# A recurrent cell and a gated network on one core: the order of the first loads, splits and bias rows

## The chip, the cores and the metric

The kernel runs on one core of one Trainium2 chip. The metric is the device time in microseconds (us) of one execution, the median of several runs. Engines are named as in the profile: PE is TensorE (PEld its weight loads), DVE is VectorE, ACT is ScalarE, POOL is GpSimd, SP is SyncE, which here only issues transfers. SPq and ACTq are the instruction queues of SP and ACT, where their transfers are issued.

## The reference

A gated recurrent cell (GRU) runs over 32 steps of a batch of 128 rows with 256 features; each of its states goes through a gated network whose weights are quantised to three levels, and the result is added to the input.

```python
def cell(h, x):
    gi = x @ W_ih + b_ih
    gh = h @ W_hh + b_hh
    i_r, i_z, i_n = jnp.split(gi, 3, axis=-1)
    h_r, h_z, h_n = jnp.split(gh, 3, axis=-1)
    r = jax.nn.sigmoid(i_r + h_r)
    z = jax.nn.sigmoid(i_z + h_z)
    n = jnp.tanh(i_n + r * h_n)
    h_new = (1.0 - z) * n + z * h
    return (h_new, h_new)
_, hs = jax.lax.scan(cell, cond, swapaxes(x, 0, 1))    # 32 steps
...
gate, up = split(hs @ ternary(w_gate_up).T)            # 256 -> 2 x 1024
hn = rms_norm(silu(gate) * up)
out = x + hn @ ternary(w_proj).T                       # 1024 -> 256
```

## The kernel before

**The work.** Step t needs the state of step t-1, so the steps form one chain. Float32 accuracy comes from split operands: each matrix is rounded to a high part (by a copy on ACT: `wi_hi`, `wh_hi`, `xT_hi`, `st_hi`), and the rest is subtracted into a low part (`wi_lo`, `wh_lo`, `xT_lo`, `st_lo`, on DVE or POOL). A product is three matmul passes: high by high, low by high, high by low. Each pass has two matmuls, since the 256 features lie in two halves of 128. The input weights W_ih are 256 x 768 (reset r, update z and candidate n, 256 columns each), and so are the state weights W_hh. `wi` and `wh` are the places in SBUF into which they are loaded (the trace calls both `work`), in the order r, n, z (`GATES`), 256 KB for each gate of each matrix.

**Biases.** Two rows of the two bias vectors are loaded (`b_rows`, inside a part of `xT_all` that is filled later), summed for r and z on DVE, rounded on ACT into `b_hi` (the trace calls that place `hid_lo`), and split on DVE into `b_split`. A matmul of `neg_ones` with `b_split` then writes a bias into a PSUM bank: `seed_rz` or `bias_rows(..., RZ, ...)` is one matmul of 512 columns, `seed_n` two of 256 (L1039).

**The start.** PE first runs `busy(10)`, ten matmuls of 512 columns on zeros whose result nobody reads. Then step 0 is computed gate by gate: `first_input(i)` multiplies the first input with gate i's W_ih, `first_state(i)` the first state with its W_hh. `cT` is the transposed first state as loaded; its high part is copied by ACT, its low part is subtracted by DVE (L885, semaphore `c_lo`). The waits are semaphores: `wi_hi_ok` and `wh_hi_ok` for the high parts of the weights, `wi_ok` and `wh_ok` for the low ones, `wh_z_ok` for the low part of W_hh's z columns, which POOL makes (L327), and `b_split_ok`, which is 1 when the candidate's bias rows are there and 2 when those of r and z are.

**Steps 0 to 7** (`LEAD` = 8) run before any product of the gated network. In each, PE computes the state products of r, n and z, then the bias and input products of the next step (`seed_rz`, `input_rz`, `input_n_part`), and then transposes the new state in two halves (`ps_t`, `hT_early`). Odd steps use the bank `ps_ffn[2]` for r and z, even ones `ps_rz`. Between the gate functions ACT takes pieces of the quantisation of the network's weights, `q_abs_of(u)` and others, for six blocks u of 512 KB; `ld_w[u]` tells that a block has landed. After step 8 the network's products fill PE between the steps.

**Order.** Every engine's program is written out by hand, and each engine takes its instructions in order. Transfers are issued by SP in the order of its program (biases, six weight pieces, inputs, blocks) and two by ACT (L542 the first input, L543 the first state).

## Time and profile before

| what | us |
|---|---|
| median of 3 runs | 345.35 (344.94 to 345.5) |
| the profiled execution: its own time | 345.16 |
| its span, from the first instruction to the last | 343.4 |
| PE busy | 338.2 (98% of the span) |
| DVE busy | 233.1 (68%) |
| ACT busy | 224.9 (66%) |
| POOL busy | 184.1 (54%) |

The profiled execution took 1.76 us more than its span, and it was 0.19 us shorter than the median. A busy PE is not the same as a PE at its full speed: what a matmul costs is read from the distance of its start to the next one's. The row PEclk of the page shows a granted clock of nine tenths or more in all slices, and a mean of 1.000, but the spacing of the matmuls in the first microseconds is twice that of the later ones, which is the spacing of the lower of the two clocks, 1.2 GHz.

### The profile page before, as it was taken

Reading aid. Unit: us, or ns where it says so; the run is one execution under the profiler, and the core shown is the slowest. Engines: PE = TensorE matmul, PEld = TensorE weight load, DVE = VectorE, ACT = ScalarE, POOL = GpSimd, SP = SyncE. Lnnn points to the kernel's source line nnn. Section 1 sums busy time; section 2 is a strip of 40 time slices with the busy share of each in tenths; the row PEclk is TensorE's granted clock in tenths of the full one; section 3 lists DMA queues with packets and bytes.
Section 4 is the critical chain, followed back from the end, with each engine's and each line's share of the span. In section 5 each row is a group of like instructions: output and inputs, shape, how many; then the busy total and the mean of one; then the engine's idle time right before and its main releaser. Section 6 shows DMA issues by size and latency. Waiting matters only on the chain.

```text
span 343.4 us, 5618 instructions
## 1 busy us (share of the span) xinstructions
PE 338.2 (98%) x2048; PEld 294.4 (86%) x2053; DVE 233.1 (68%) x462; ACT 224.9 (66%) x442; POOL 184.1 (54%) x156
## 2 busy tenths in 40 slices
PE   8999999999999999999999999999999999999996
PEld 4989988888988889888888889888888888888895
DVE  7588787999576556754678554775658555665866
ACT  6778888787755757555766666566565655756662
POOL 2316571465825536255454447454462555799694
PEclk9999999999999999999999999999999999999999
DMA  7995000054001000130001000010000100010101
GB/s 241 299 402 224 2 0 2 0 186 183 1 2 62 2 0 0 71 115 2 0 0 63 0 2 1 1 63 0 2 0 15 48 1 2 0 64 1 59 4 61
DMA packets 7891, 18.72 MB, mean 55 GB/s; under 512 B 564, under 2 KB 4788, under 8 KB 7352
## 3 DMA queue, kind: packets, MB, share of 16 engines
q1 hardware_dynamic: 7176, 17.97, 14.1%
q10 hardware_dynamic: 688, 0.39, 0.4%
q8 instruction: 16, 0.26, 0.3%
q14 instruction: 11, 0.09, 0.1%
HBM read 14.17 MB, written 4.19 MB: 53 GB/s over the span
## 4 chain that ended last, share of the span: by engine, by line
PE 90%; DVE 5%; issue 2%; ACT 1%; DVEq 0%
PE ps_ffn L1126 29%; PE ps_out L1164 16%; PE ps_rz L1028 6%; PE ps_rz L1033 6%; PE ps_rz L1029 6%; PE ps_n L1028 3%; PE ps_n L1033 3%; PE ps_n L1029 3%; PE ps_rz L1126 2%; PE ps_t L1119 1%; PE ps_ffn L1291 1%; PE ps_n L1077 1%; PE ps_ffn L1028 1%; PE ps_ffn L1033 1%; PE ps_ffn L1029 1%
## 5 line engine op out<-in xcount | busy, mean ns | idle before, releaser
L359 POOL TENSOR_TENSOR hid_lo<-work,hid_hi 128x512 fp32r<-128x512 f32 x62 | 81.6, 1316 | 103.5 <-ACT hid_hi L457 99.5
L1126 PE MATMUL ps_ffn<-st_hi,wguT 128*128 128x512 f32 x236 | 93.8, 397 | 0.1
L1126 PE MATMUL ps_ffn<-st_lo,wguT 128*128 128x512 f32 x236 | 92.6, 393 | 0.0
L366 POOL TENSOR_TENSOR sq_sum<-sq_sum,work 128x512 f32<-128x512 f32 x55 | 73.2, 1331 | 1.7 <-ACT work L471 0.6
L748 DVE TENSOR_TENSOR work<-work,ps_ffn 128x512 f32<-128x512 f32 x55 | 37.6, 683 | 31.4 <-ACT work L453 31.3
L457 ACT CAST hid_hi<-work 128x512 fp32r<-128x512 f32 x63 | 38.8, 616 | 23.4 <-DVE work L758 23.4
L1126 PEld LDWEIGHTS ps_ffn<-st_hi,wguT 128*128 128x128 f32 x236 | 44.4, 188 | 8.3 <-DVE work L748 0.7
L1126 PEld LDWEIGHTS ps_ffn<-st_lo,wguT 128*128 128x128 f32 x236 | 44.5, 189 | 7.3
L758 DVE TENSOR_TENSOR work<-work,ps_ffn 128x512 f32<-128x512 f32 x63 | 43.2, 686 | 4.7 <-PE ps_ffn L1126 2.8
L1164 PEld LDWEIGHTS ps_out<-wpT,hid_hi 128*128 128x128 f32 x240 | 35.8, 189 | 3.7
L1164 PE MATMUL ps_out<-wpT,hid_lo 128*128 128x256 f32 x240 | 38.8, 284 | 0.0
L421 ACT ACTIVATE rz<-ps_rz 128x512 f32<-128x512 f32 x24 | 14.3, 596 | 36.9 <-PE ps_rz L1033 36.8
L1164 PE MATMUL ps_out<-wpT,hid_hi 128*128 128x256 f32 x240 | 38.3, 282 | 0.0
L453 ACT ACTIVATE work<-ps_ffn 128x512 f32<-128x512 f32 x55 | 32.3, 587 | 6.8 <-PE ps_ffn L1126 6.5
L687 DVE TENSOR_TENSOR r_hn<-rz,ps_n 128x256 f32<-128x256 f32 x28 | 11.7, 419 | 35.6 <-PE ps_n L1033 35.1
L471 ACT ACTIVATE work<-work 128x512 f32<-128x512 f32 x55 | 34.6, 629 | 0.0
L1164 PEld LDWEIGHTS ps_out<-wpT,hid_lo 128*128 128x128 f32 x240 | 33.0, 191 | 0.4 <-POOL hid_lo L359 0.4
L1028 PE MATMUL ps_rz<-wi_hi,xT_hi 128*128 128x512 f32 x54 | 21.4, 396 | 0.0
L1029 PE MATMUL ps_rz<-wi_lo,xT_hi 128*128 128x512 f32 x54 | 21.2, 392 | 0.0
L322 POOL TENSOR_TENSOR xT_lo<-xT_all,xT_hi 128x256 fp32r<-128x256 f32 x10 | 8.1, 814 | 22.2 <-ACT rz L413 20.0
L1028 PE MATMUL ps_rz<-wh_hi,st_hi 128*128 128x512 f32 (+1 forms) x52 | 19.8, 383 | 0.0
L1029 PE MATMUL ps_rz<-wh_lo,st_hi 128*128 128x512 f32 (+1 forms) x52 | 19.7, 381 | 0.0
(232 smaller groups left out, 713.7 us busy)
## 6 DMA issues: line engine op xcount, KB each, us to landing
out_dram<-o_st SPq DMA_DIRECT2D x7, 512.0 KB, 2.8
xT_all<-in_x_dram SPq DMA_DIRECT2D x1, 3072.0 KB, 16.4
x_ring<-in_x_dram SPq DMA_DIRECT2D x1, 3072.0 KB, 11.2
x_ring<-in_L_ffn_w_gate_up_dram SPq DMA_DIRECT2D x4, 512.0 KB, 9.5
x_ring<-in_L_ffn_w_proj_dram SPq DMA_DIRECT2D x2, 512.0 KB, 11.7
x_ring<-in_x_dram SPq DMA_DIRECT2D x1, 1024.0 KB, 6.0
work<-in_L_cond_W_ih_dram SPq DMA_DIRECT2D x3, 256.0 KB, 4.5
work<-in_L_cond_W_hh_dram SPq DMA_DIRECT2D x3, 256.0 KB, 4.8
```

The costliest lines, as they stand in the source:

```text
L359: nc.gpsimd.tensor_tensor(hid_lo[:, j % RING], hid[:, j % 2], f32(hid_hi[:, j % RING]), ALU.subtract).then_inc(hid_lo_ok, 1)
L366: nc.gpsimd.tensor_tensor(sq_sum[:], sq_sum[:], hid_sq[:, j % 2], ALU.add).then_inc(sq_added, 1)
L453: nc.scalar.activation(sg[:, j % 2], gate_bank(G, j), ACT.Sigmoid).then_inc(sg_ok, 1)
L457: nc.scalar.copy(hid_hi[:, j % RING], hid[:, j % 2]).then_inc(hid_hi_ok, 1)
L471: nc.scalar.activation(hid_sq[:, j % 2], hid[:, j % 2], ACT.Square).then_inc(hid_sq_ok, 1)
L748: nc.vector.tensor_tensor(gsg[:, j % 2], sg[:, j % 2], gate_bank(G, j), ALU.mult).then_inc(gsg_ok, 1)
L758: nc.vector.tensor_tensor(hid[:, j % 2], gsg[:, j % 2], up_bank(G, j), ALU.mult).then_inc(hid_ok, 1)
L1028: pe.matmul(dst, hi[:, k, :], w_hi[:, k, cols], start=False, stop=False, skip_group_check=True)
L1029: pe.matmul(dst, hi[:, k, :], w_lo[:, k, cols], start=False, stop=False, skip_group_check=True)
L1033: mm = pe.matmul(dst, lo[:, k, :], w_hi[:, k, cols], start=False, stop=stop and k == KD - 1, skip_group_check=True)
L1126: mm = pe.matmul(bank, w, group_state(part, G, k), start=(k == 0 and i == 0), stop=(k == KD - 1 and i == 1))
L1164: mm = pe.matmul(ps_out[:, s, :], part[:, j % RING, s * P:(s + 1) * P], wpT[:, j, :], start=(j == 0 and s % 2 == 0 and part is hid_hi), st ...
```

## The change

- SP's first transfer is W_ih's r columns; the transposed first state `cT` comes second, then the other weights as before. The two bias loads move from the head of SP's program to ACT's, behind the first input; `cT` leaves ACT's.
- On ACT the copy of W_ih's r columns goes ahead of the rounding of the r and z bias.
- On DVE the split of the r and z bias goes behind the low part of W_ih's r columns. The low part of the first state moves from DVE to POOL.
- On PE there are eight matmuls on zeros in place of ten. The candidate's bias (`seed_n(0)`) moves into `first_input(0)`, ahead of the pass that needs `wi_lo`; the bias of r and z moves into `first_state(0)`, ahead of the pass that needs `wh_lo`. The bias of r and z for step 2 (`seed_rz(2)`, bank `ps_rz`) moves from behind step 1's products to ahead of step 0's transposes, with a wait on `rz_ok` (ACT has read step 0's z).

```diff
@@ block.sync
                 for to, w, landed in ((wi, w_ih, ld_wi), (wh, w_hh, ld_wh)):
                     sp.dma_start(to[:, :, GATES[i]],
                                  w.rearrange("(k p) n -> p k n", p=P)[:, :, GATES[i]]).then_inc(landed[i], 16)
+                    if i == 0 and to is wi:
+                        sp.dma_start(cT[:], cond_t.rearrange("(k p) b -> p k b", p=P)).then_inc(ld_cT, 16)
...
-            for i, b in enumerate((b_ih, b_hh)):
-                sp.dma_start(b_rows[:, i * G3:(i + 1) * G3], b.partition_broadcast(2)).then_inc(ld_b, 16)
             for i in range(3):
                 load_gate(i)
@@ block.gpsimd
             input_lo(0)
+            pool.wait_ge(h_hi, 1)
+            nc.gpsimd.tensor_tensor(state(st_lo, -1), cT[:], f32(state(st_hi, -1)), ALU.subtract).then_inc(c_lo, 1)
             pool.wait_ge(wh_hi_ok, 3)
@@ block.scalar
             act.dma_start(xT_all[:, :, 0:1, :], xt[:, :, 0:1, :]).then_inc(ld_x0, 16)
-            act.dma_start(cT[:], cond_t.rearrange("(k p) b -> p k b", p=P)).then_inc(ld_cT, 16)
+            for i, b in enumerate((b_ih, b_hh)):
+                act.dma_start(b_rows[:, i * G3:(i + 1) * G3], b.partition_broadcast(2)).then_inc(ld_b, 16)
...
             nc.scalar.copy(both_n(b_hi), both_n(b_all)).then_inc(b_hi_ok, 1)
+            w_ih_hi(0)
             act.wait_ge(b_sum_ok, 1)
             nc.scalar.copy(b_hi[:, RZ], b_all[:, RZ]).then_inc(b_hi_ok, 1)
-            w_ih_hi(0)
             act.wait_ge(ld_cT, 16)
@@ block.vector
-            dve.wait_ge(b_hi_ok, 2)
-            nc.vector.scalar_tensor_tensor(out=b_split[0:2, RZ], in0=f32(b_hi[:, RZ]), scalar=ident[0:2, 1:2],
-                                           in1=b_all[:, RZ], op0=ALU.mult, op1=ALU.subtract).then_inc(b_split_ok, 1)
...
             w_ih_lo(0)
-            dve.wait_ge(h_hi, 1)
-            nc.vector.tensor_tensor(state(st_lo, -1), cT[:], f32(state(st_hi, -1)), ALU.subtract).then_inc(c_lo, 1)
+            dve.wait_ge(b_hi_ok, 2)
+            nc.vector.scalar_tensor_tensor(out=b_split[0:2, RZ], in0=f32(b_hi[:, RZ]), scalar=ident[0:2, 1:2],
+                                           in1=b_all[:, RZ], op0=ALU.mult, op1=ALU.subtract).then_inc(b_split_ok, 1)
             w_hh_lo(0)
@@ block.tensor, first_input
+                if i == 0:
+                    pe.wait_ge(b_split_ok, 1)
+                    seed_n(0)
                 pe.wait_ge(wi_ok, i + 1)
@@ block.tensor, first_state
+                if i == 0:
+                    pe.wait_ge(b_split_ok, 2)
+                    bias_rows(ps_rz[:], RZ, False)
                 if i == 1:
                     seed_rz(1)
@@ block.tensor
-            busy(10)
+            busy(8)
             pe.wait_ge(consts, 5)
             first_input(0, ps_rz[:, 0:D])
-            pe.wait_ge(b_split_ok, 2)
-            bias_rows(ps_rz[:], RZ, False)
             first_state(0, ps_rz[:, 0:D], r_sum)
-            seed_n(0)
...
-                    seed_rz(t + 1)
+                    if t > 1:
+                        seed_rz(t + 1)
                     input_rz(t + 1)
...
                 input_n_part(t + 1, 0)
+                if t == 0:
+                    pe.wait_ge(rz_ok, 1)
+                    seed_rz(2)
                 for k, (ready, done) in enumerate(((h_left, hT_left), (h_ok, hT))):
```

PE at the start of the program, from the matmuls on zeros to the last pass of the r gate, in the kernel before (line, operation, output and inputs, shape of the output):

```order
L1291 MATMUL ps_ffn<-q_keep 128x512 x10
L1302 MATMUL ps_rz<-wi_hi,xT_hi 128x256 x2
L1302 MATMUL ps_rz<-wi_hi,xT_lo 128x256 x2
L1306 MATMUL ps_rz<-wi_lo,xT_hi 128x256 x2
L1039 MATMUL ps_rz<-b_split,neg_ones 128x512
L1317 MATMUL ps_rz<-wh_hi,st_hi 128x256 x2
L1317 MATMUL ps_rz<-wh_hi,st_lo 128x256 x2
L1329 MATMUL ps_rz<-wh_lo,st_hi 128x256 x2
L1039 MATMUL ps_n<-b_split,neg_ones 128x256 x2
```

The same place in the changed kernel:

```order
L1291 MATMUL ps_ffn<-q_keep 128x512 x8
L1302 MATMUL ps_rz<-wi_hi,xT_hi 128x256 x2
L1302 MATMUL ps_rz<-wi_hi,xT_lo 128x256 x2
L1039 MATMUL ps_n<-b_split,neg_ones 128x256 x2
L1309 MATMUL ps_rz<-wi_lo,xT_hi 128x256 x2
L1320 MATMUL ps_rz<-wh_hi,st_hi 128x256 x2
L1320 MATMUL ps_rz<-wh_hi,st_lo 128x256 x2
L1039 MATMUL ps_rz<-b_split,neg_ones 128x512
L1335 MATMUL ps_rz<-wh_lo,st_hi 128x256 x2
```

The two bias writes have moved: the candidate's from the end to the fourth place, that of r and z from the fifth to the eighth.

ACT at the start of the program, before:

```order
L542 DMA xT_all<-in_x_dram 128x2x128
L543 DMA cT<-in_cond_dram 128x2x128
L545 ACT_TABLE_LOAD
L545 ACTIVATE table<-ones 128x1
L449 CAST xT_hi<-xT_all 128x256
L549 CAST hid_lo<-xT_all 2x2x256
L551 CAST hid_lo<-xT_all 2x512
L535 CAST wi_hi<-work 128x2x256
L554 CAST st_hi<-cT 128x2x128
L539 CAST wh_hi<-work 128x2x256
```

and in the changed kernel:

```order
L544 DMA xT_all<-in_x_dram 128x2x128
L546 DMA xT_all<-in_L_cond_b_ih_dram 2x768
L546 DMA xT_all<-in_L_cond_b_hh_dram 2x768
L548 ACT_TABLE_LOAD
L548 ACTIVATE table<-ones 128x1
L451 CAST xT_hi<-xT_all 128x256
L552 CAST hid_lo<-xT_all 2x2x256
L537 CAST wi_hi<-work 128x2x256
L555 CAST hid_lo<-xT_all 2x512
L557 CAST st_hi<-cT 128x2x128
L541 CAST wh_hi<-work 128x2x256
```

ACT issues three transfers in place of two ahead of its table load, and the copy of W_ih's r columns stands ahead of the second bias rounding (L551 before, L555 now).

PE at step 0's transposes, as a difference (with - the kernel before, with + the changed one; L1366 and L1373 are the same line of code):

```order
 L1077 MATMUL ps_ffn<-wi_hi,xT_hi 128x256
 L1077 MATMUL ps_ffn<-wi_lo,xT_hi 128x256
-L1366 MATMUL ps_t<-ident,h_nat 128x128
+L1039 MATMUL ps_rz<-b_split,neg_ones 128x512
+L1373 MATMUL ps_t<-ident,h_nat 128x128
 L1077 MATMUL ps_ffn<-wi_hi,xT_hi 128x256
 L1077 MATMUL ps_ffn<-wi_lo,xT_hi 128x256
```

One matmul of 512 columns now stands between step 1's input products and the first transpose; the same matmul is gone from behind `q_group_sums` in step 1.

## Rows read from the trace of the kernel before

**Rows 1.** The page: busy us (share) by engine; the chain that ended last, by engine.

```profile
PE 338.2 (98%) x2048; PEld 294.4 (86%) x2053; DVE 233.1 (68%) x462; ACT 224.9 (66%) x442; POOL 184.1 (54%) x156
...
PE 90%; DVE 5%; issue 2%; ACT 1%; DVEq 0%
```

**Rows 2.** PE's timeline, 0 to 14 us: start, duration, engine, line, what, count.

```profile
1.45 4.45 PE L1291 MATMUL ps_ffn<-q_keep 128*128 128x512 bf16 x10 [1.45 <-DVE q_keep L856]
5.92 0.77 PE L1302 MATMUL ps_rz<-wi_hi,xT_hi 128*128 128x256 f32 x2
...
6.86 0.40 PE L1306 MATMUL ps_rz<-wi_lo,xT_hi 128*128 128x256 f32 x2
7.09 0.39 PE L1039 MATMUL ps_rz<-b_split,neg_ones 128*128 128x512 f32 x1
7.32 0.40 PE L1317 MATMUL ps_rz<-wh_hi,st_hi 128*128 128x256 f32 x2
...
8.02 0.40 PE L1039 MATMUL ps_n<-b_split,neg_ones 128*128 128x256 f32 x2
8.26 0.40 PE L1302 MATMUL ps_n<-wi_hi,xT_hi 128*128 128x256 f32 x2
...
11.81 0.40 PE L1329 MATMUL ps_rz<-wh_lo,st_hi 128*128 128x256 f32 x2
```

**Rows 3.** ACT's timeline, 0 to 14 us.

```profile
3.98 0.61 ACT L551 CAST hid_lo<-xT_all 2x512 fp32r<-2x512 f32 x1
5.16 0.62 ACT L535 CAST wi_hi<-work 128x512 fp32r<-128x512 f32 x1 [0.57 <-DMA work<-in_L_cond_W_ih_dram]
5.68 0.40 ACT L554 CAST st_hi<-cT 128x256 fp32r<-128x256 f32 x1
6.22 0.62 ACT L539 CAST wh_hi<-work 128x512 fp32r<-128x512 f32 x1
...
12.53 1.05 ACT L511 ACTIVATE q_abs<-x_ring 128x1024 bf16<-128x1024 f32 x1
13.83 0.27 ACT L446 CAST st_hi<-ps_t 128x128 fp32r<-128x128 f32 x1 [0.26 <-PE ps_t L1366]
```

**Rows 4.** DVE's and POOL's timelines, 0 to 14 us.

```profile
3.12 0.68 DVE L862 TENSOR_TENSOR xT_all<-xT_all 2x512 f32<-2x512 f32 x1 [0.80 <-DMA xT_all<-in_L_cond_b_hh_dram]
...
6.88 0.69 DVE L880 TENSOR_TENSOR wh_lo<-work,wh_hi 128x512 fp32r<-128x512 f32 x1
...
3.63 0.76 POOL L322 TENSOR_TENSOR xT_lo<-xT_all,xT_hi 128x256 fp32r<-128x256 f32 x1 [1.03 <-ACT xT_hi L449]
9.94 1.29 POOL L327 TENSOR_TENSOR wh_lo<-work,wh_hi 128x512 fp32r<-128x512 f32 x1 [5.56 <-ACT wh_hi L539]
```

**Rows 5.** SP's timeline: its first transfer and that of W_ih's r columns.

```profile
0.73 0.36 SPq L268 DMA_DIRECT2D xT_all<-in_L_cond_b_ih_dram  x1
...
1.44 0.41 SPq L261 DMA_DIRECT2D work<-in_L_cond_W_ih_dram  x1
```

**Rows 6.** DMA issues at 1.44, 1.89 and 5.98 us: size, us from issue to landing.

```profile
work<-in_L_cond_W_ih_dram SPq DMA_DIRECT2D x1, 256.0 KB, 3.7
...
work<-in_L_cond_W_hh_dram SPq DMA_DIRECT2D x1, 256.0 KB, 4.3
...
x_ring<-in_L_ffn_w_gate_up_dram SPq DMA_DIRECT2D x1, 512.0 KB, 6.5
```

**Rows 7.** Windows: PE, PEld, DVE, ACT, POOL busy, PEclk, DMA share, GB/s.

```profile
3.00:3.50 0.50, 0.50 (x2) 0.15 (x1) 0.38 (x1) 0.49 (x4) 0.00 (x0) 1.00 0.63 164
...
4.50:5.00 0.50, 0.50 (x3) 0.21 (x2) 0.50 (x2) 0.09 (x1) 0.00 (x0) 1.00 0.95 295
```

**Rows 8.** Transposes of steps 0 and 1 on PEld, step 1's new state on DVE.

```profile
13.46 0.14 PEld L1366 LDWEIGHTS ps_t<-ident,h_nat 128*128 128x128 f32 x1 [0.31 <-DVE h_nat L728]
...
18.74 0.14 PEld L1366 LDWEIGHTS ps_t<-ident,h_nat 128*128 128x128 f32 x1
...
18.14 0.48 DVE L715 TENSOR_TENSOR h_nat<-zh,ps_ffn 128x128 f32<-128x128 f32 x2
```

## The prediction
> **What bounds the kernel now.** First the page: PE is busy for 98% of the span, and 90% of the chain that ended last runs through PE [rows 1]. So a microsecond of order on another engine counts only where PE waits for it, and a matmul counts only where it stands in PE's line. The change touches step 0 and two places of steps 0 and 1, so the second view is PE's timeline of the first 14 us [rows 2]. The reader is to see three stretches. From 1.45 us PE works on zeros, ten matmuls in 4.45 us, 0.43 us each. From 5.92 us it does real work, still at that pace (0.21 us for 256 columns); the pair at 6.86 us is the first whose successor starts after 0.23 us, so there the clock rose from 1.2 to 2.4 GHz, although PE had not stood still for more than 0.2 us since 1.45. After that a pair of 256 columns, or one matmul of 512, costs 0.23 to 0.24 us, and I find no gap until the transposes. What starts the real work is seen on ACT: it idled 0.57 us for W_ih's r columns and copied them from 5.16 to 5.78 us [rows 3]; PE followed 0.14 us later. The columns were issued at 1.44 us [rows 5] and took 3.7 us to land [rows 6], that is at 5.14.
>
> The third view answers where PE waits later [rows 8]. Before step 0's first transpose the weight loads idled 0.31 us for DVE's new state. Before step 1's (18.74 us) nothing idled. There the new state was ready earlier: in step 0 PE could start 0.34 us after DVE's pair began (its rows at 13.12 and 13.46 us, of which the second is shown), and in step 1 that pair began at 18.14, so 18.48 was possible and 18.74 was used. Step 1 is bound by PE, with 0.26 us in hand.
>
> **The bias row of step 2.** It is one matmul of 512 columns, 0.23 us by the distance from 7.09 to 7.32 us [rows 2]. Taken out of step 1, it makes PE arrive 0.23 us sooner at the transposes, within the 0.26 us in hand: a gain of 0.23. Put in step 0, it fills 0.23 of the 0.31 us in which the loads idled: cost 0 to 0.05 us, I take 0. Its new wait is for ACT's reading of z, which comes before DVE can make the state and so is always over first.
>
> **The start of the real work.** W_ih's r columns go from 1.44 to 0.73 us [rows 5]. If they land as fast as before, at 4.43, that is 0.71 us of gain, provided ACT is free. ACT now issues three transfers ahead of its table load, some 0.15 us more than two. The bias loads landed 1.97 us after the second one's issue at 1.15 (DVE was let go at 3.12 [rows 4]); issued near 1.6 they land near 3.6, and the first rounding ends its turn near 4.2, still ahead of 4.43. The second rounding (0.61 us [rows 3]) now stands behind the copy, in time in which ACT would wait for W_hh: it takes 4.95 to 5.5, `st_hi` 5.5 to 5.8, and W_hh's r columns, which landed at 1.89 + 4.3 = 6.19, come at 5.8 to 6.0. So PE's first real matmul moves from 5.92 to about 5.2. The eight matmuls on zeros end at 1.45 + 8 x 0.43 = 4.9, so the dropped two cost nothing and would otherwise have stood in the way until 5.75.
>
> **What of that reaches the end of step 0.** PE then works at the lower clock until about 6.85 us, if the clock rises where it did. From 5.2 that is 1.65 us or 7.7 matmuls of 256 columns at 0.213. It has exactly eight to do that need no W_hh: four of the first input, two of the candidate's bias, two with `wi_lo`. They end near 6.9. W_hh's copy, 6.22 to 6.84 before, ends by then at 6.5 to 6.6, so `st_hi`, `st_lo` and the bias of r and z follow at once, 0.7 us; `wh_lo`, ready at 7.57 before [rows 4] and 0.25 to 0.3 earlier now, is there for the last pair. That ends near 7.83, and the candidate's input products start, which before started at 8.26 [rows 2]. Gain: 0.43. With W_ih landing at 4.2 and PE starting at 5.05 it is 0.55; I take **0.48**, inside the two. The same work is done in the same number of matmuls; what is won is that 0.7 us more of it is done before W_hh is ready.
>
> **What must follow.** Each later wait of step 0 must have this much in hand. POOL's `wh_lo` for z ends at 11.23 [rows 4] and is used at 11.81 [rows 2]: 0.58 in hand, plus what the loads gain. POOL also has the first state's low part now, some 0.76 us for 128 x 256 by its row at 3.63 [rows 4] against 0.42 on DVE; from 5.8 to 6.6, before PE asks for it at 7.1 and three us before POOL's next work: 0. DVE's own line only exchanges that for a bias split. The tightest is ACT: `q_abs_of(0)` needs the first block of the gate and up weights, issued at 5.98 and landed 6.5 us later, at 12.48 [rows 6], and ACT started it at 12.53; it holds ACT for 1.05 us, and then `st_hi` of step 0 had 0.26 us in hand [rows 3]. So the gain of step 0 can be no more than 0.26 plus what this block gains. That gain is between the idle time that the earlier issue fills and the issue time: the DMA engines were busy for a share of 0.63 in 3.0 to 3.5 us and of 0.95 in 4.5 to 5.0 [rows 7], which is 0.16 us lost in the one window alone, and SP issues everything after `cT` 0.2 us sooner. I take 0.25, bounds 0.15 and 0.4. The cap is 0.51, and 0.48 passes.
>
> **The sum.** 0.48 + 0.23 = 0.71 us off the profiled execution's 345.16, 344.45. That execution lies 0.19 below the median, so against the median of 345.35 the forecast is 344.65. Nothing behind step 1 is tied to the clock on the wall: the 3 MB of inputs is issued at 16.8 us and used past 40, and the rest of the loads waits for the work itself.
>
> The Trainium skill (DMA: Bandwidth & Descriptors, "Issuing engines are not separate DMA queues") says that transfers issued from two engines share the same 16 DMA engines, so that a second issuer saves only the time of issuing. By this W_ih's r columns now compete with the first input, which was alone in front before. The bytes ahead of their landing fall only by `cT`, 128 KB, and at the 295 KB per us of the window at 4.5 us that is 0.45 us instead of 0.71. PE would start at 5.47, and by the count above the gain of step 0 would be 0.3, the time 344.8. No row here shows the two side by side.
>
> **The rivals.** (1) Most of the gain of step 0 is caught by the loads: W_ih's r columns share the engines with the first input and land near 4.9, or the block for `q_abs_of(0)` comes no sooner. For it: the transfers from 5 us on ran at full share [rows 7]. Against it: the idle share before that. With 0 to 0.3 left, plus 0.23: 344.85 to 345.1. (2) More comes: the clock rises earlier than 5.9 in the typical run, so that PE waits for data alone, or the loads gain 0.4. Then step 0 gains 0.6 to 0.65 and the time is 344.5. (3) Slower: the clock. Between the last zero matmul (4.9) and the first real one PE now stands for 0.3 us or more, and what follows may have holes too. If W_ih's copy comes no sooner than before, the hole is 1 us. If the clock then rises later than 6.85, each us at 1.2 GHz costs 0.5 us of work; from 1.4 us of delay on the gain is gone, and if the clock stayed low once more for the 5.4 us that it did in this trace, 2.7 us would be lost: 346.0 to 347.3. For it: in the trace the clock rose only after 5.4 us of almost unbroken work. Against it: the total of matmuls before 6.85 stays nearly the same.
>
> The Trainium skill (TensorE: Matmul & The Clock Gate, Part 1) says that the point at which the clock rises shifts between runs of the same kernel, depending on where its first matmul falls. The two traces could then differ there by chance; the medians less so. The sum by it would be 0.64 to 0.82, the same within my range.
>
> **How the numbers follow.** The forecast (344.5 to 344.85) has 0.60, rival 1 0.22, rival 2 0.10, rival 3 0.08. About 0.2% of the time, 0.69 us, is what a measurement of this kernel can tell from no change, and my forecast of 0.70 lies at that line. A little over half of its 0.60 counts as faster, with all of rival 2 and little else: faster 0.45. Same: the rest of the forecast and rival 1, 0.48. Slower 0.07, rival 3. The range leaves out rival 3 and the ends: 344.3 to 345.2.
>
> **What would show it.** In the profile of the changed kernel: PE's first real matmul at 5.0 to 5.3 us; its pairs at 0.43 us until the clock rises, then no gap before 7.1; the candidate's input products near 7.8; step 0's first transpose near 13.0 and without the 0.31 us; step 1's near 18.0. Wrong would be: ACT's copy of W_ih's r columns after 4.8 (rival 1), `st_hi` of step 0 waiting behind `q_abs_of(0)`, POOL's low part of the state after 7.1, or pairs at 0.43 us behind 7 us (rival 3).

## The result, and the profile after

The changed kernel takes 346.78 us, the median of 5 runs (346.53 to 347.07), against 345.35 for the kernel before in 5 runs beside it. The ratio is 1.0042, 95% interval 1.0023 to 1.0062: it is slower, by 1.4 us, where 0.7 us faster was forecast. The profiled execution took 346.78 us, of which 344.6 are its span and 2.18 lie outside. Before it was 345.16, with a span of 343.4 and 1.76 outside. So 1.2 us were lost inside the span and 0.4 outside. One profiled execution in this document, that of a_busy10_dve_memset, ran at a granted clock of 0.62 and took 501.58 us; it is left out of that kernel's numbers in the table below, which are those of the nine others.

The page's span, PE's line and the chain that ended last, in the kernel after (compare [rows 1]):

```profile
span 344.6 us, 5614 instructions
...
PE 90%; DVE 4%; issue 2%; ACT 2%; DMA 1%; ACTq 0%; DVEq 0%
```

PE bounds the kernel as before. New in the chain is DMA with 1%: it now runs through the landing of the second bias vector, and from there over ACT to PE's first real matmul at 6.09 us (start, us, what):

```profile
1.87 2.92 DMA xT_all<-in_L_cond_b_hh_dram
...
4.81 0.62 ACT hid_lo L552
5.43 0.53 ACT wi_hi L537
```

Where the time goes is told by one group in two kernels, the transposes of the state that L1119 does from step 8 on (number of them, min/median/max ns, start of the first and of the last). Before:

```profile
L1119 PE MATMUL ps_t<-ident,h_nat x48: 271/273/273, 55.9 to 288.8; 128*128 128x128 f32 x48
```

After:

```profile
L1119 PE MATMUL ps_t<-ident,h_nat x48: 271/272/273, 57.2 to 290.1; 128*128 128x128 f32 x48
```

The first is 1.3 us later and the last is 1.3 us later. So what was lost inside the span was lost before step 8, and after it nothing more was lost or given back. PE's timeline of the first 14 us in the kernel after, to be read against [rows 2]:

```profile
1.45 3.59 PE L1291 MATMUL ps_ffn<-q_keep 128*128 128x512 bf16 x8 [1.45 <-DVE q_keep L859]
6.09 0.77 PE L1302 MATMUL ps_rz<-wi_hi,xT_hi 128*128 128x256 f32 x2 [1.05 <-ACT wi_hi L537]
6.66 0.63 PE L1302 MATMUL ps_rz<-wi_hi,xT_lo 128*128 128x256 f32 x2
...
9.22 0.65 PE L1335 MATMUL ps_rz<-wh_lo,st_hi 128*128 128x256 f32 x2
9.68 0.43 PE L1302 MATMUL ps_n<-wi_hi,xT_hi 128*128 128x256 f32 x2
9.95 0.40 PE L1302 MATMUL ps_n<-wi_hi,xT_lo 128*128 128x256 f32 x2
...
13.26 0.40 PE L1335 MATMUL ps_rz<-wh_lo,st_hi 128*128 128x256 f32 x2
```

The level of the clock is read here and below from the spacing, 0.43 us a pair for the lower and 0.23 to 0.24 for the higher; the granted clock in the windows of these microseconds is 1.00 at both. The reader is to see three things. The real work begins at 6.09 us, not at 5.2 as forecast and not even at 5.92 as before. Ahead of it PE stood for 1.05 us, from the end of the eight zero matmuls. And all real matmuls of the r gate then run at the lower clock, 0.43 us for a pair, up to 9.7 us, where before the clock rose at 6.86. The candidate's input products start at 9.68 instead of 8.26, which is 1.42 us late, and the last pass of z is 1.45 late. Why `wi_hi` came late is on ACT:

```profile
4.26 0.40 ACT L451 CAST xT_hi<-xT_all 128x256 fp32r<-128x256 f32 x1 [0.62 <-DMA xT_all<-in_x_dram]
4.81 0.62 ACT L552 CAST hid_lo<-xT_all 2x512 fp32r<-2x512 f32 x1
5.33 0.61 ACT L537 CAST wi_hi<-work 128x512 fp32r<-128x512 f32 x1
6.05 0.62 ACT L555 CAST hid_lo<-xT_all 2x512 fp32r<-2x512 f32 x1
6.58 0.40 ACT L557 CAST st_hi<-cT 128x256 fp32r<-128x256 f32 x1
6.88 0.61 ACT L541 CAST wh_hi<-work 128x512 fp32r<-128x512 f32 x1
```

and in the first transfers of SP and ACT (start, us of issuing) and their landings (KB, us from issue to landing; SP's W_ih columns, ACT's first input):

```profile
0.73 0.44 SPq L261 DMA_DIRECT2D work<-in_L_cond_W_ih_dram  x1
0.74 0.50 ACTq L544 DMA_DIRECT2D xT_all<-in_x_dram  x1
...
1.87 0.24 ACTq L546 DMA_DIRECT2D xT_all<-in_L_cond_b_hh_dram  x1
...
work<-in_L_cond_W_ih_dram SPq DMA_DIRECT2D x1, 256.0 KB, 3.3
xT_all<-in_x_dram ACTq DMA_DIRECT2D x1, 128.0 KB, 3.5
```

W_ih's columns were there at 0.73 + 3.3 = 4.03 us, 1.1 us sooner than before. But the first input, which before was copied from 3.14 us on, landed only at 4.24, and the biases near 4.8 instead of 3.1. ACT takes them in its order: the first input, the candidate's bias, and only then W_ih's columns, which had waited for 1.3 us. So the transfer that was put first came sooner, and nothing could start with it. (No kernel here copies W_ih's columns ahead of the first input and the bias.) DVE and POOL beside that, in the kernel after (compare [rows 4]):

```profile
4.81 1.20 DVE L865 TENSOR_TENSOR xT_all<-xT_all 2x512 f32<-2x512 f32 x1 [2.49 <-DMA xT_all<-in_L_cond_b_hh_dram]
...
7.21 1.22 DVE L884 SCALAR_TENSOR_TENSOR b_split<-hid_lo,ident,xT_all 2x512 fp32r<-2x512 f32 x1
8.36 0.67 DVE L879 TENSOR_TENSOR wh_lo<-work,wh_hi 128x512 fp32r<-128x512 f32 x1
...
4.74 0.73 POOL L322 TENSOR_TENSOR xT_lo<-xT_all,xT_hi 128x256 fp32r<-128x256 f32 x1 [2.13 <-ACT xT_hi L451]
7.05 0.83 POOL L327 TENSOR_TENSOR st_lo<-cT,st_hi 128x256 fp32r<-128x256 f32 x1 [1.58 <-ACT st_hi L557]
```

The sum of the biases took 1.20 us where it took 0.68, and the second split 1.22. Both ran while POOL subtracted, and each ended 0.54 or 0.55 us after POOL had: 6.01 after 5.47, 8.43 after 7.88. `wh_lo` is 1.5 us later than before (8.36 for 6.88).

What worked as forecast is the bias row of step 2. The transposes of steps 0 and 1 on PEld, after (compare [rows 8]):

```profile
14.90 0.14 PEld L1373 LDWEIGHTS ps_t<-ident,h_nat 128*128 128x128 f32 x1 [0.19 <-DVE h_nat L731]
...
19.94 0.14 PEld L1373 LDWEIGHTS ps_t<-ident,h_nat 128*128 128x128 f32 x1
```

Step 0's is 1.44 us late, step 1's only 1.20: 0.24 was won between them. How much of that a kernel gets depends on what PE finds ahead of step 0's transposes; see b_seed_only below.

### The profile page after: what moved, and what is told of

It is laid out like the page before. It is cut to its first block, busy times and chain, and to the rows that moved or that the text cites. A ratio compares the mean times of both kernels' runs of the same rounds, so it can differ in the third digit from the quotient of the medians.

```text
span 344.6 us, 5614 instructions
## 1 busy us (share of the span) xinstructions
PE 338.5 (98%) x2046; PEld 295.0 (86%) x2051; DVE 233.2 (68%) x461; ACT 224.9 (65%) x442; POOL 185.0 (54%) x157
## 4 chain that ended last, share of the span: by engine, by line
PE 90%; DVE 4%; issue 2%; ACT 2%; DMA 1%; ACTq 0%; DVEq 0%
PE ps_ffn L1126 29%; PE ps_out L1164 16%; PE ps_rz L1028 6%; PE ps_rz L1033 6%; PE ps_rz L1029 6%; PE ps_n L1028 3%; PE ps_n L1033 3%; PE ps_n L1029 3%; PE ps_rz L1126 2%; PE ps_t L1119 1%; PE ps_ffn L1033 1%; PE ps_n L1077 1%; PE ps_ffn L1028 1%; PE ps_ffn L1029 1%; DMA xT_all<-in_L_cond_b_hh_dram 1%
## 5 line engine op out<-in xcount | busy, mean ns | idle before, releaser
L690 DVE TENSOR_TENSOR r_hn<-rz,ps_n 128x256 f32<-128x256 f32 x28 | 11.7, 418 | 35.3 <-PE ps_n L1033 35.1
```

## The experiments

"Before" and "after" are the two kernels; each kernel below is one of them with the edit shown. The kernels of one batch ran on one chip, each batch on another, and share runs of the kernel before, whose median was 345.23, 345.22, 345.24, 345.08 and 345.55 us in the five batches. Where two kernels of different batches are compared below, a tenth or two of their difference may be the chips'. "Outside" is the time of an execution less its span, the median over a kernel's executions; in the kernel before it was 1.8.

| kernel | batch | median us (runs) | ratio to before, 95% interval | span of the profiled one | outside |
|---|---|---|---|---|---|
| a_busy10 | 1 | 346.53 (11) | 1.0037 [1.0026, 1.0049] | 344.4 | 2.15 |
| b_busy8 | 1 | 346.45 (12) | 1.0027 [1.0009, 1.0045] | 345.0 | 1.80 |
| a_loads_before | 1 | 346.86 (10) | 1.0043 [1.0025, 1.0061] | 345.5 | 2.17 |
| b_seed_only | 1 | 345.07 (12) | 1.0004 [0.9987, 1.0022] | 343.1 | 1.83 |
| a_busy10_clo_dve | 2 | 346.04 (8) | 1.0026 [1.0016, 1.0036] | 344.3 | 1.82 |
| b_clo_pool | 2 | 345.54 (12) | 1.0016 [1.0005, 1.0026] | 343.4 | 2.17 |
| b_loads_after | 2 | 347.84 (4) | 1.0079 [1.0066, 1.0092] | 346.3 | 1.79 |
| a_loads_before_busy10_clo_dve | 2 | 345.22 (11) | 1.0003 [0.9993, 1.0013] | 343.3 | 1.84 |
| after_again | 3 | 347.27 (6) | 1.0054 [1.0040, 1.0068] | 345.1 | 2.19 |
| order_wih_first | 3 | 345.74 (11) | 1.0014 [1.0005, 1.0022] | 344.0 | 1.83 |
| b_seed_seedn | 3 | 344.71 (12) | 0.9988 [0.9980, 0.9996] | 343.1 | 1.81 |
| b_pool_memset | 3 | 344.74 (11) | 0.9984 [0.9976, 0.9993] | 343.1 | 1.80 |
| b_clo_pool_dve_memset | 4 | 345.31 (11) | 1.0010 [1.0001, 1.0018] | 344.0 | 1.81 |
| b_pool_sub_small | 4 | 345.14 (11) | 1.0004 [0.9995, 1.0012] | 343.5 | 1.81 |
| b_tile_only | 4 | 344.70 (11) | 0.9991 [0.9978, 1.0004] | 342.7 | 1.80 |
| b_seed_seedn_tile | 4 | 344.49 (12) | 0.9989 [0.9976, 1.0002] | 345.1 | 1.79 |
| a_busy10_dve_memset | 5 | 346.16 (9) | 1.0023 [1.0014, 1.0033] | 344.3 | 1.81 |
| b_seed_seedn_tile_2 | 5 | 344.30 (6) | 0.9967 [0.9955, 0.9979] | 342.6 | 1.83 |

### The zero matmuls and the clock

**a_busy10** is the kernel after with the ten zero matmuls back, **b_busy8** the kernel before with eight.

```diff
-            busy(8)
+            busy(10)
```

> The changed kernel with ten matmuls on zeros again in place of eight, nothing else. Theory 1 (the hole): in the changed kernel PE stood idle from 5.04 to 6.09 us, and its clock rose only near 9.7 us instead of 6.85, which is 2.8 us more at half speed, 1.4 us lost. Ten matmuls end near 5.9, the hole is 0.2 us as in the kernel before, the pairs go to 0.23 us spacing near 7 us and the time is 345.1 to 345.4. Theory 2 (the loads): the splits of step 0 come late because the first input and the biases land 1.1 and 1.7 us later, and PE would stand behind them at either clock: 346.5 to 346.8, with PE gaps before 9 us.

> The kernel before with eight matmuls on zeros in place of ten, loads and order untouched. Theory 1: the hole is 5.04 to 5.92 us, the clock rises 3 us later, step 0 ends 1.3 to 1.5 us later: 346.6 to 346.9. Theory 2: nothing changes, since the real work waits for W_ih's columns until 5.92 in both: 345.3.

PE's timeline in a_busy10:

```profile
1.45 4.34 PE L1291 MATMUL ps_ffn<-q_keep 128*128 128x512 bf16 x10 [1.45 <-DVE q_keep L859]
6.08 0.47 PE L1302 MATMUL ps_rz<-wi_hi,xT_hi 128*128 128x256 f32 x2 [0.29 <-ACT wi_hi L537]
...
9.38 0.40 PE L1302 MATMUL ps_n<-wi_hi,xT_hi 128*128 128x256 f32 x2
```

and in b_busy8:

```profile
6.28 0.77 PE L1302 MATMUL ps_rz<-wi_hi,xT_hi 128*128 128x256 f32 x2 [1.23 <-ACT wi_hi L535]
...
9.40 0.57 PE L1039 MATMUL ps_n<-b_split,neg_ones 128*128 128x256 f32 x2
9.81 0.40 PE L1302 MATMUL ps_n<-wi_hi,xT_hi 128*128 128x256 f32 x2
```

With ten, the hole is 0.29 us and PE has its higher clock from the first real pair on (0.47 us, and the next pair 0.31 later). With eight, a hole of 1.23 us is followed by some 3.4 us at the lower clock. In b_busy8 five executions took 344.8 to 345.4 us and seven 346.4 to 347.3, while of the 32 of the kernel before beside them one reached 347.2, and of all its 142 in this document two. So two zero matmuls fewer do not cost time in each execution; they make those that take 1.2 to 2.1 us more than the five's median of 345.2 more frequent. That all seven had the late clock is an inference: only one of them was profiled (346.84), and there W_ih's columns came 0.36 us later than in [rows 3] as well. In the kernel after the price is 0.25 (346.78 against 346.53) to 0.74 (**after_again**, 347.27, the same kernel in batch 3, where the pairs stayed at 0.43 us until 10.6; 346.6 to 346.8 was expected). The intervals of all three overlap, so the 0.25 is not told from nothing by the medians; in the profiles the candidate's products start 0.30 us apart.

> The changed kernel once more, beside the three others on one chip. If its parts add up as measured so far (late loads about 0.8 us, POOL's instruction 0.36 us outside the span, eight matmuls on zeros 0.1 to 0.3 us), 346.6 to 346.8 and 2.15 us outside the span in every run.

But with ten zero matmuls and the clock up, the kernel after is still 1.3 us slower than before. After 6.4 us PE waits again and again in a_busy10 (of the pairs at 6.68, 7.29, 7.89, 8.44 and 9.04 us each next one starts 0.34 to 0.61 us later, not 0.24), and the candidate's products start at 9.38, only 0.3 sooner. The clock is the smaller part.

### Transfers against order

**a_loads_before** is the kernel after with the transfers of the kernel before; **b_loads_after** is the kernel before with those of after, the reverse of the edit shown.

```diff
             for i, b in enumerate((b_ih, b_hh)):
-                act.dma_start(b_rows[:, i * G3:(i + 1) * G3], b.partition_broadcast(2)).then_inc(ld_b, 16)
+                sp.dma_start(b_rows[:, i * G3:(i + 1) * G3], b.partition_broadcast(2)).then_inc(ld_b, 16)
...
-                    if i == 0 and to is wi:
-                        sp.dma_start(cT[:], cond_t.rearrange("(k p) b -> p k b", p=P)).then_inc(ld_cT, 16)
...
+            act.dma_start(cT[:], cond_t.rearrange("(k p) b -> p k b", p=P)).then_inc(ld_cT, 16)
```

> The changed kernel with the transfers issued as in the kernel before (biases first on SP, first state on ACT); the new order on ACT, DVE, POOL and PE and the eight matmuls on zeros stay. The first input and the biases should land near 3.1 us again. Theory 1: PE still waits for W_ih's columns until 5.9, the hole is 0.9 us, the clock rises late: 346.4 to 346.8. Theory 2: with the loads back the loss is gone: 344.9 to 345.2.

> The kernel before with the transfers issued as in the changed one, nothing else. Theory 2 (the loads): the first input lands at 4.2 instead of 3.1 us and the biases at 4.8 instead of 3.1; DVE's sum takes 1.17 us beside POOL and ends at 5.95, ACT's second rounding ends at 6.6 and only then comes the copy of W_ih's r columns, 1.4 us later than before: 346.4 to 346.8. If the early W_ih columns were worth more than the late biases: below 345.

b_loads_after is the slowest of all, by 2.6 us over before (four executions, 347.67 to 348.12), a full us more than was expected. Its PE:

```profile
7.37 0.47 PE L1303 MATMUL ps_rz<-wi_hi,xT_hi 128*128 128x256 f32 x2 [1.47 <-ACT wi_hi L535]
...
8.94 0.40 PE L1318 MATMUL ps_rz<-wh_hi,st_lo 128*128 128x256 f32 x2
9.18 0.59 PE L1330 MATMUL ps_rz<-wh_lo,st_hi 128*128 128x256 f32 x2
...
12.83 0.40 PE L1303 MATMUL ps_rz<-wi_hi,xT_hi 128*128 128x256 f32 x2
```

In the old order of ACT both bias roundings stand ahead of W_ih's copy, so the late biases hold it until 6.6 us. That is the early part of the loss; the rest is the clock, which shows a second form here: it is high from 7.37 to 9.2, then falls to the lower level for 3.4 us, although PE has worked without a gap since 8.5, and rises again. a_loads_before showed the same after its hole of 1.29 us (high from 6.33, low from 8.2 to 11.7), and so it said nothing on the transfers: eight zero matmuls spoiled it, since its time of 346.86 fitted the theory of the late clock and could not exclude the other. The next pair is without that.

**a_busy10_clo_dve** is after with ten zero matmuls and the subtraction of `c_lo` on DVE, behind the bias split; **a_loads_before_busy10_clo_dve** has the old transfers as well, so that only the order on ACT, DVE and PE is new.

```diff
-            pool.wait_ge(h_hi, 1)
-            nc.gpsimd.tensor_tensor(state(st_lo, -1), cT[:], f32(state(st_hi, -1)), ALU.subtract).then_inc(c_lo, 1)
...
+            dve.wait_ge(h_hi, 1)
+            nc.vector.tensor_tensor(state(st_lo, -1), cT[:], f32(state(st_hi, -1)), ALU.subtract).then_inc(c_lo, 1)
             w_hh_lo(0)
```

> The changed kernel with ten matmuls on zeros and with the low part of the first state back on DVE, behind the bias split. Theory 2a (DVE and POOL collide): in the run with ten matmuls DVE's sum and its second split of the bias rows took 1.17 and 1.22 us instead of 0.68 and 0.73, each while POOL subtracted; with POOL out of the second, the split is 0.73 us, but DVE has 0.42 us more to do, so the r gate ends about as before and the span stays within 0.15 us of 344.4. Theory 3 (outside the span): the changed kernel spends 2.15 us outside its span and the kernel before 1.80, and so does every variant with POOL's additional instruction; if that instruction is the cause, this one shows 1.80 and comes out near 346.1. Theory 2 without the collision: 346.5.

> The changed kernel's order on ACT, DVE and PE alone: the transfers as in the kernel before, ten matmuls on zeros, first state's low part on DVE. What is left of the change is the copy of W_ih's columns ahead of the second bias rounding, the two bias writes of step 0 moved on PE, and the bias row of step 2. Theories 2 and 3: no late load, no collision, no time outside: at most the kernel before, less 0.23 us for the row of step 2 if that gain is real: 344.9 to 345.2. If the second rounding and split, now on ACT's and DVE's line between the weights, delay W_hh's parts by 0.3 us: 345.3 to 345.5.

PE in a_busy10_clo_dve, and then PE and DVE in a_loads_before_busy10_clo_dve:

```profile
9.41 0.40 PE L1302 MATMUL ps_n<-wi_hi,xT_hi 128*128 128x256 f32 x2
```

```profile
8.41 0.40 PE L1301 MATMUL ps_n<-wi_hi,xT_hi 128*128 128x256 f32 x2
...
7.34 0.67 DVE L876 TENSOR_TENSOR wh_lo<-work,wh_hi 128x512 fp32r<-128x512 f32 x1
```

The new transfers cost 346.04 - 345.22 = 0.82 us with all else equal and the clock up in both profiles, where the candidate's products start 1.00 us apart. The new order as a whole neither costs nor gains anything that can be told from zero (ratio 0.9993 to 1.0013, or -0.2 to +0.4 us).

**order_wih_first** is that last kernel with one change: W_ih's r columns are issued by SP ahead of the biases, which stay on SP.

```diff
+                    if i == 0 and to is wi:
+                        for j, b in enumerate((b_ih, b_hh)):
+                            sp.dma_start(b_rows[:, j * G3:(j + 1) * G3], b.partition_broadcast(2)).then_inc(ld_b, 16)
...
-            for i, b in enumerate((b_ih, b_hh)):
-                sp.dma_start(b_rows[:, i * G3:(i + 1) * G3], b.partition_broadcast(2)).then_inc(ld_b, 16)
```

> The kernel with the changed order and the transfers of before that gave 345.22, with one thing moved: W_ih's r columns are issued ahead of the two biases, all three on SP; the first input and the first state stay on ACT. Theory 2b (it is the 256 KB of W_ih beside the first input that make the input and the biases late, not which queue issues the biases): the first input lands near 4.2 us and the biases near 4.5, and the time is 345.8 to 346.1. Theory 2c (the biases were late because they stood behind the first input in ACT's queue): both land before 3.7, W_ih near 4.4, and the time is 344.7 to 345.1.

It is 0.5 us slower than the one without that change, and its ACT, DVE and POOL show why:

```profile
4.31 0.41 ACT L450 CAST xT_hi<-xT_all 128x256 fp32r<-128x256 f32 x1 [1.03 <-DMA xT_all<-in_x_dram]
...
4.62 0.68 DVE L863 TENSOR_TENSOR xT_all<-xT_all 2x512 f32<-2x512 f32 x1 [2.30 <-DMA xT_all<-in_L_cond_b_hh_dram]
5.36 1.08 DVE L866 SCALAR_TENSOR_TENSOR b_split<-hid_lo,ident,xT_all 2x512 fp32r<-2x512 f32 x1
...
4.80 1.08 POOL L323 TENSOR_TENSOR xT_lo<-xT_all,xT_hi 128x256 fp32r<-128x256 f32 x1 [2.19 <-ACT xT_hi L450]
```

The first input is as late as in the kernel after (4.31), though nothing but the 256 KB was put beside it: its landing takes 3.5 us instead of 2.4. The biases, on SP's queue as before and issued 0.5 us later, came 1.5 us later (4.62 for 3.12). So it is not ACT's queue that delays them. What changed ahead of them are W_ih's 256 KB, and, since the second bias is now issued at 1.62 us and `cT` at 1.26, the 128 KB of `cT` too; the two were not separated.

### The first state's low part on POOL

**b_clo_pool** is the kernel before with the subtraction on POOL.

```diff
+            pool.wait_ge(h_hi, 1)
+            nc.gpsimd.tensor_tensor(state(st_lo, -1), cT[:], f32(state(st_hi, -1)), ALU.subtract).then_inc(c_lo, 1)
             pool.wait_ge(wh_hi_ok, 3)
...
-            dve.wait_ge(h_hi, 1)
-            nc.vector.tensor_tensor(state(st_lo, -1), cT[:], f32(state(st_hi, -1)), ALU.subtract).then_inc(c_lo, 1)
```

> The kernel before with the low part of the first state on POOL in place of DVE, nothing else. Theory 3: the span is as before, 343.3, since PE asks for that part late enough, but 2.15 us lie outside it instead of 1.80: 345.55 to 345.6. Theory 2a: POOL's work from 6.1 to 6.9 us meets DVE's low part of W_hh and makes that 1.1 us long instead of 0.69, PE waits 0.2 to 0.3 us for it: span 343.6. Neither: 345.2.

It is 0.32 us slower with the same span, and all 12 executions had 2.13 to 2.23 us outside it where the kernel before has 1.8. In the span most of DVE's gain is eaten, DVE and POOL in b_clo_pool:

```profile
6.39 1.00 DVE L882 TENSOR_TENSOR wh_lo<-work,wh_hi 128x512 fp32r<-128x512 f32 x1
...
5.91 0.93 POOL L327 TENSOR_TENSOR st_lo<-cT,st_hi 128x256 fp32r<-128x256 f32 x1 [1.59 <-ACT st_hi L556]
```

The subtraction of 0.42 us is off DVE, and `wh_lo` takes 1.00 instead of 0.69, ending at 7.39, again 0.55 after POOL's end at 6.84. Four kernels narrow down where the 0.36 us outside come from: a memset of one column on POOL; the same on DVE in place of the subtraction moved to POOL; a small subtraction on POOL behind the same wait; and the memset on DVE in the kernel after with ten zero matmuls. Nobody reads what they write.

```diff
@@ b_pool_memset
+        scratch = sb("scratch", [P, 1])
...
+            nc.gpsimd.memset(scratch[:], 0.0)
             pool.wait_ge(wh_hi_ok, 3)
@@ b_clo_pool_dve_memset and a_busy10_dve_memset, where the subtraction was
+            nc.vector.memset(spare[:], 0.0)
@@ b_pool_sub_small
+            pool.wait_ge(h_hi, 1)
+            nc.gpsimd.tensor_tensor(spare[:], cT[:, 0, :32], f32(state(st_hi, -1))[:, 0, :32], ALU.subtract)
             pool.wait_ge(wh_hi_ok, 3)
```

> The kernel before with one more instruction on POOL, a memset of one column into a tile that nobody reads, behind its first low part. Theory 3: any further instruction in POOL's program costs the 0.36 us outside the span: 2.17 us outside, 345.55. Rival 3a: it was the subtraction with its wait, not the number: 1.80 outside, 345.2.

> The kernel before with the subtraction of the first state's low part on GpSimd, and in its place on VectorE a memset of one column into a tile that nothing reads, so that both engines carry at least as many instructions as in the kernel before. With GpSimd's subtraction alone the profiled execution had 2.17 us outside its span instead of 1.81. Theory 3a (the 0.36 us outside the span come with the instruction that GpSimd has more): 2.15 to 2.2 outside, about 345.5. Theory 3b (they come with the instruction that VectorE has fewer): 1.8 to 1.85 outside, about 345.2.

> The kernel before with a small subtraction (32 columns) on GpSimd behind the same wait for the state's high part, its result read by nobody, VectorE unchanged. Theory 3a (what GpSimd has more, a subtraction that waits for ScalarE, puts 0.36 us outside the span): 2.15 to 2.2 outside, 345.5. Theory 3b (VectorE's missing instruction does it): 1.8 to 1.85 outside, 345.2. If both this and its neighbour show 1.8, only the large subtraction on GpSimd or both changes together do it.

> The changed kernel with its ten zero matmuls back and a memset of one column on VectorE where the change took the subtraction out (its result is read by nobody). The same kernel without the memset took 346.53, with 2.16 us outside the span. Theory 3b (the 0.36 us outside the span come with VectorE's missing instruction): 1.8 to 1.85 outside and 346.1 to 346.3, the span unchanged near 344.4, since VectorE's longer operations are still there. Its rival (the changed kernel has them for another reason than the kernel before with that move alone): 2.15 to 2.2 and 346.5.

One instruction more on POOL leaves 1.8 outside, with or without the wait. The large subtraction on POOL leaves 1.8 too as soon as DVE has an instruction in its place. So the 0.36 us need DVE's missing instruction, and that holds in the kernel after as well: 346.16 for 346.53, with the span as it was (344.3 for 344.4). Whether they need POOL's large subtraction too is open, since no kernel here has one DVE instruction fewer without it. What happens in those 0.36 us lies outside the profile, and stays open too.

### The bias rows on PE, and a tile

**b_seed_only** is the kernel before with `seed_rz(2)` moved as in the change; **b_seed_seedn** moves `seed_n(0)` too, but leaves the bias of r and z of step 0 where it was; **b_tile_only** has a tile of one column that nothing uses; **b_seed_seedn_tile** has all three, and was run twice.

```diff
@@ b_seed_only, b_seed_seedn
-                    seed_rz(t + 1)
+                    if t > 1:
+                        seed_rz(t + 1)
...
+                if t == 0:
+                    pe.wait_ge(rz_ok, 1)
+                    seed_rz(2)
@@ b_seed_seedn, in first_input and behind first_state(0, ...)
+                if i == 0:
+                    pe.wait_ge(b_split_ok, 1)
+                    seed_n(0)
                 pe.wait_ge(wi_ok, i + 1)
...
-            seed_n(0)
@@ b_tile_only
         ones = sb("ones", [P, 1])
+        scratch = sb("scratch", [P, 1])
```

> The kernel before with one thing moved: the bias row of r and z for step 2 goes ahead of step 0's transposes. Both theories: it fills 0.23 of the 0.31 us in which PE waited for DVE, and step 1 is 0.23 us shorter: 345.1. If the transposes of step 0 are pushed by as much as step 1 gains, 345.35.

> The kernel before with two moves on PE and nothing else: the bias row of step 2 ahead of step 0's transposes, and the candidate's bias of step 0 ahead of the pass that needs W_ih's low part. Theory: the first gives 0.2 us; the second gives another 0.24 in runs where the clock rose before 5.9 us, since PE then waits for that low part, and nothing where it rose near 6.9: 344.8 to 345.0. Rival: the second only moves the wait to W_hh, whose columns land when they land: 345.05 as with the first move alone.

> The kernel before with one unused tile of a column allocated where the memset kernel had it, and no instruction more: every later tile lies 4 bytes further on in each partition. Theory 4a (the memset kernel was 0.5 us faster, 344.74, because the tiles behind lie elsewhere): 344.6 to 344.9. Theory 4b (it was the instruction on GpSimd, or which chip ran it): 345.1 to 345.4.

> The kernel before with the two moves of bias rows on TensorE (step 2's bias row of r and z behind step 1's new gate, step 0's bias row of n ahead of the first W_ih products; 344.71 alone) and the unused tile. Theory 4a: both gains add, 344.1 to 344.4, the fastest of all. Theory 4b: 344.6 to 344.9, as without the tile.

> The same kernel as b_seed_seedn_tile again, on what may be another chip, to tell its ratio to the kernel before (0.9989, interval to 1.0002) from 1: 344.3 to 344.6 and a ratio of 0.998 to 0.999 if the two moves on TensorE and the tile are what made it faster, 345 if it was chance.

`seed_rz(2)` alone gives 0.16 us in the medians, which is not told from zero by its interval. Its profile shows why it gives less than 0.24: there PE's weight loads waited 0.34 us, up to 12.36, for `xT_lo` (POOL's subtraction took 0.97 us beside DVE's `zh`) and came to step 0's transposes without idle time, so that the bias row was not hidden; the distance to step 1's transposes is 5.15 us, against 5.28 before and 5.04 after. Both moves give 0.53, and that is told from zero: ratio 0.9988. With the tile it is 344.49 and 344.30, the second time clear of noise (ratio 0.9967), and the fastest of all kernels here. The tile alone gave 0.38, and the memset on POOL, which brought the same tile, 0.50. The tile moves every later one by 4 bytes. The interval of the tile alone still holds 1, but the profiles show more than the medians. In b_tile_only the 48 transposes from step 8 on are at:

```profile
L1120 PE MATMUL ps_t<-ident,h_nat x48: 270/272/273, 55.6 to 288.1; 128*128 128x128 f32 x48
```

From the first to the last it is 232.5 us, where it is 232.9 before and after. In all four kernels with that tile it is 232.5 to 232.6, in the fifteen others 232.8 to 232.9 (a_busy10_dve_memset is left out), also in the two of these that have an unused tile behind all the others. So some 0.3 us of the gain come in steps 8 to 31 and go with where tiles lie. No view here shows which instruction gets faster, and why it does is not shown.

The profile of b_seed_seedn_tile was an execution with a late clock, 346.93 us, while eleven others took 344.1 to 345.2. Its ACT and PE:

```profile
5.87 0.62 ACT L536 CAST wi_hi<-work 128x512 fp32r<-128x512 f32 x1 [1.32 <-DMA work<-in_L_cond_W_ih_dram]
...
6.64 0.77 PE L1303 MATMUL ps_rz<-wi_hi,xT_hi 128*128 128x256 f32 x2 [0.74 <-ACT wi_hi L536]
...
10.98 0.40 PE L1310 MATMUL ps_n<-wi_lo,xT_hi 128*128 128x256 f32 x2
```

and PE of the same kernel in b_seed_seedn_tile_2:

```profile
5.76 0.47 PE L1303 MATMUL ps_rz<-wi_hi,xT_hi 128*128 128x256 f32 x2
...
8.21 0.40 PE L1310 MATMUL ps_n<-wi_lo,xT_hi 128*128 128x256 f32 x2
```

In one execution W_ih's columns landed 0.7 us later than before, PE stood 0.74 us behind its ten zero matmuls, and the pairs were at 0.43 us until about 10.6: the candidate's `wi_lo` pass is 2.8 us later, and the whole 2.5. The same kernel without a hole had the high clock at 5.76. So what b_busy8's edit does can also come by chance, with a late transfer.

## Why the prediction was wrong

The 1.4 to 2.0 us come apart into four terms, each the difference of two kernels' distances from the kernel before of their own batch: new order 0.00, new transfers +0.82, `c_lo` on POOL +0.48 (0.33 of it outside the span), eight zero matmuls +0.13 to +0.73. That they add up to the 1.43 and 2.03 us of the kernel after in its two measurements proves nothing, since each difference begins at the kernel at which the last one ends. The transfers are the largest term that is clear of noise; the order of the terms could shift some tenths between them. Step by step:

**"W_ih's r columns go from 1.44 to 0.73 us"** and land at 4.43: right, and sooner than forecast, 4.03. The prediction's second estimate, 0.45 us of gain by the bytes ahead (landing near 4.7), erred on the other side. ACT's third transfer was put at 0.15 us and cost 0.42 (its table load starts at 2.14 instead of 1.72), which did not matter: ACT then idled 0.62 us for the first input.

**"The bias loads ... issued near 1.6 they land near 3.6"**: this failed, and it is the step that decided. The forecast had ACT free for the copy of W_ih's r columns at 4.2; it came to it at 5.33. The second bias was issued at 1.87 and took 2.9 us, and so let DVE go at 4.8. The 1.97 us of landing was read from a trace in which 128 KB and one bias of 6 KB had been issued ahead, and was carried to one in which W_ih's 256 KB, `cT`'s 128 KB and W_hh's 256 KB (at 1.73) had been as well. The first input was not costed at all. I took its copy at 3.14 for given, though the first input now had W_ih's 256 KB beside it, and it landed at 4.24. The windows of the kernel after show where that time is (columns as in [rows 7]):

```profile
2.00:2.50 0.50, 0.50 (x3) 0.15 (x1) 0.32 (x2) 0.36 (x1) 0.39 (x2) 1.00 0.48 139
...
3.00:3.50 0.50, 0.50 (x2) 0.15 (x1) 0.00 (x0) 0.49 (x2) 0.00 (x0) 1.00 1.13 357
```

From 3.0 us the engines are full, 357 KB per us where before they moved 164 [rows 7], which is the idle share that I had meant to use. What used it was W_ih's columns and what stands behind them, at the cost of 140 KB that were needed first. The Trainium skill (DMA: Bandwidth & Descriptors, "Issuing engines are not separate DMA queues") says that transfers interleave on the same 16 DMA engines whichever engine issued them. The runs agree: in order_wih_first, with the biases on SP's queue, the second took 3.0 us to land, and 2.9 from ACT's in the kernel after. I weighed it for the large transfer only. It was the small ones that paid.

**"The dropped two cost nothing"**: failed. They bridged the wait until the first copy. The forecast had the hole at 0.3 us; since the start came at 6.09, it was 1.05. That condition stood in rival 3 ("If W_ih's copy comes no sooner than before, the hole is 1 us"), and two of the forecast's own signs of being wrong came true, the copy after 4.8 and pairs at 0.43 us behind 7. Rival 3's size of 346.0 to 347.3 holds the result, but by luck: it was made of the clock alone, and with the clock up a_busy10 still takes 346.53. Its chance of 0.08 was too small, since I left out the loads that make the hole. The Trainium skill (TensorE: Matmul & The Clock Gate, Part 1) says that the rise shifts between runs of one kernel. The two profiles of b_seed_seedn_tile agree, with the higher clock from 5.76 and from about 10.6. What it adds up to is not chance alone, though, as the share of executions above 346.3 us went from 1 of 32 to 7 of 12 in b_busy8.

**"DVE's own line only exchanges that for a bias split"**, POOL at 0: failed twice. The exchange leaves DVE 0.49 us longer in the split, which is what the subtraction took away (0.42), and the bias split now stands ahead of `wh_lo`. In every trace here each DVE instruction of 512 columns with both inputs in SBUF that started during one of POOL's subtractions ended 0.53 to 0.58 us after it (the `zh` of step 0, 256 columns, 0.27 to 0.41): 1.20, 1.22, 1.00 and 1.08 us in the rows shown, for work that takes 0.67 to 0.73 us otherwise. `r_hn` and `n_pre`, which read PSUM, kept their 0.42 us beside it. With POOL silent (a_busy10_clo_dve) the split took 0.73. The Trainium skill (SBUF — State Buffer, "Who interferes with whom") states this as a lock: a VectorE instruction with two inputs in SBUF and a GpSimd instruction that reads SBUF contend for a shared port, which one of them holds while the other waits. The rows agree, in the other direction too: in order_wih_first POOL's subtraction started behind DVE's and took 1.08 us, where it takes 0.72 or 0.73 with DVE idle. The 0.76 of [rows 4], by which the forecast priced it, has a little of this wait in it. I had looked up what POOL's instruction costs and not what it does to its neighbour. The 0.36 us outside the span could not have been read from any row.

**"They end near 6.9"**, and step 0 gains 0.43 to 0.55: failed. The r gate is the same work in the same number of matmuls, but all of it ran at the lower clock, from 6.09 to 9.68, so the arithmetic of the forecast and of rival 1 fell with its start. The clock's rise at 6.86 was also one trace's: in nine of the other profiles with ten zero matmuls the higher clock is there from the first real pair. With the old transfers and the new order (a_loads_before_busy10_clo_dve) the candidate's products start 3.32 us after ACT began to copy W_ih's r columns (8.41 and 5.09), and 2.73 in b_seed_seedn (7.68 and 4.95), which has two of PE's three moves and nothing of ACT's and DVE's. So these two moves were worth 0.53 us in the medians, and the rest of the new order took it back. What did is argued and not tested by itself: on ACT the second rounding stands ahead of W_hh's copy (6.44 us, and 5.78 in b_seed_seedn), and on DVE the second split stands ahead of `wh_lo` (7.34, and 6.54).

**The cap by ACT's `q_abs_of(0)`** was not tested in the kernel after, since nothing came early enough.

**The bias row of step 2**: right in mechanism and size in the kernel after, 0.24 in the traces against 0.23; in the kernel before alone it gave 0.13 by the same distance.

## What to carry to other kernels

A large transfer that is put first can delay the small ones that share its moment, here from either queue; list what the first instruction of each engine needs, and let those bytes go ahead of the large ones. Dummy matmuls ahead of the first real one should reach up to it: count them to the latest arrival of the data, not to the expected one. Before work goes from VectorE to GpSimd, look at what VectorE does in the same microsecond: here a VectorE instruction with two SBUF inputs that met GpSimd's subtraction waited for it each time. Two moves on PE alone were worth 0.5 us; the rest of the change was worth less than nothing.

## What the runs showed of the hardware that was not expected

- With one VectorE instruction fewer in the whole program, moved to GpSimd, 0.36 us more lie between the span and the execution's time: 2.11 to 2.24 in each of the 44 executions of such kernels, 1.75 to 1.89 in all others. A memset of one column on VectorE in its place takes that away. The cause is open.
- The clock, as read from the spacing, can fall again while PE works. In b_loads_after it was at the higher level from 7.37 to 9.2 us, behind a hole of 1.47, and then at the lower for 3.4 us. Seven profiles here have a hole of 0.74 to 1.47 us ahead of the real work. In six of them PE then ran for 3.4 to 4.4 us at 1.2 GHz, at once or after 2 us; the seventh, a_busy10_clo_dve, had the clock up before its hole of 0.92 us (its ten zero matmuls took 3.85 us instead of 4.45) and kept it. Of the twelve other profiles with ten zero matmuls and the full granted clock, none has a hole above 0.48 us, and in none is a pair still at 0.43 us after 7.2. So a hole goes with the late clock and does not decide it; what does was not found.
- With an unused tile of one column allocated among the others the stretch from step 8 on took 232.5 to 232.6 us in four profiles, against 232.8 to 232.9 in fifteen without it. The medians gained 0.4 us (tile alone, 0.9978 to 1.0004) and 0.5 (with the memset, 0.9976 to 0.9993). A difference of a tenth of a per cent between two kernels may be no more than where their tiles lie.
